# First pass of narrow attention over 64 rows of the array, two heads at a time

## The chip, the cores and the metric

The kernel runs on one core of a Trainium2 chip. The metric is the device time of one execution in microseconds (us). TensorE (PE in the rows, its weight loads PEld) does the matrix products, VectorE (DVE) the reductions, ScalarE (ACT) the exponentials, GpSimd (POOL) small work on SBUF, and SyncE (SP) issues the transfers.

## The reference

Two layers in the macaron form. Each layer has a feed-forward block, an attention block and a feed-forward block. The change touches only the two attentions with 16 heads of 8 dimensions, over 2 sequences of 1024 positions:

```python
scores = einsum('bhqd,bhkd->bhqk', q, k) / sqrt(8)      # first layer, causal
scores = where(causal, scores, -inf)
o = einsum('bhqk,bhkd->bhqd', softmax(scores), v)

att = softmax(einsum('nqd,nkd->nqk', qm, km))           # second layer, not causal
att_out = einsum('nqk,nkd->nqd', att + batch_pos, vm)
```

Everything else (the mixtures of experts, the windowed attention, the norms) is the same before and after.

## The kernel before

A head has only 8 dimensions, so q and k are each cut into three bf16 parts. The products of parts are stacked along the contraction: rows 24i to 24i+23 of `q_slot` hold part i of the queries three times, those of `k_slot` the three parts of the keys, in all 72 rows. Rows 72 to 95 are zero. Rows 96 to 98 hold ones in `k_slot`, and in `q_slot` the negated row maximum in three parts, which a first pass has to find.

Heads are worked on in 8 groups of four. A group has two halves of 512 queries. For a half there are two kinds of work:

- **The first pass.** An item is 128 queries of one head against up to 512 keys: one matmul over 96 rows into one of three banks (`m_bank`, L1463), in the causal stage for the block on the diagonal a second matmul that adds the mask (L1466), then a maximum on DVE (L1529). After the last item of a half DVE negates the maxima (L1538). A "turn" (L1458, a transpose on PE) stands some items later; DVE copies it out (L1525), POOL cuts it into three parts (L1421 to L1427), and three transfers put these into rows 96 to 98 of `q_slot` (L1381).
- **The second pass.** A unit is 128 keys of four heads against up to 512 queries: four scores over 128 rows (L1480), two exponentials on ACT (L1549), in the causal stage a clearing of the diagonal squares on POOL, and four products with the values, each into 32 columns of the array (L1495, fp32, two records each). The first scores of a half wait for the three transfers of its turn.

PE works through a list that is fixed when the program is built. `due(u)` says how many items have been issued before unit u; these are spread among the units. A prologue of items runs before the first unit (49 in the second layer's stage, 62 in the causal one, turns included). An item may be issued when the bank that it wants has been reduced: item m waits for the reductions up to m-3. DVE takes the items in the same order.

SP loads a group's slots with six transfers (`load`), groups 0 to 2 at the start into three slots, later ones when a slot comes free. It also issues `rows` (the three transfers after a turn) and `store` (the result of a half). A transfer that waits holds everything behind it on SP. Group 0 is loaded in the block ahead of the stage, and blocks end with a barrier over all engines.

In the trace the causal stage has the prefix `a1x` (its slots `a1a`), the other `b1x` (`b1a`).

Of the kernel before, what the change touches and what calls it, by code (L numbers as in the profile page):

```python
# [22 lines left out]
NC = 512  # L23
# [1087 lines left out]
class Narrow:  # L1111


    def __init__(self, phase, dram, positions_split):
# [4 lines left out]
        self.k_slot = [phase.sb(f"k_slot{s}", [128, 4, L], BF16) for s in range(3)]  # L1119
        self.v_aug = phase.sb("v_aug", [128, GROUPS, GRANULE_TILES, 128])  # L1120
# [6 lines left out]
        self.slot_loaded = [phase.sem(f"slot_loaded{s}") for s in range(SLOTS)]  # L1127

# [28 lines left out]
    def load(self, sp, group):  # L1157

        n, s = group * 4, group % SLOTS
        for i in range(PARTS):  # L1160
# [6 lines left out]
                         ).then_inc(self.slot_loaded[s], 16)  # L1167

# [113 lines left out]
def narrow_attention(nc, tag, sbuf, dram, narrow, causal):  # L1282
# [16 lines left out]
    for half in range(HALVES):  # L1299
# [5 lines left out]
        for qt in range(4 * qh, 4 * qh + 4):  # L1305
            keys = (qt + 1) * 128 if causal else L
            items += [(half, qt, hh, k0, min(NC, keys - k0)) for k0 in range(0, keys, NC) for hh in (3, 0, 1, 2)]
# [12 lines left out]
    for item in items:  # L1320
        worth.append(worth[-1] + (item[4] + 32 if item[1] is not None else 256))

    def due(u):
# [6 lines left out]
        return max(m for m in range(NI + 1) if worth[m] <= aim)  # L1330

# [10 lines left out]
    for half in range(HALVES):  # L1342
        during = max([u for u in range(NU) if dues[u] <= turn_at[half]], default=-1)
        late = during >= 0 and turn_at[half] - dues[during] >= 2
        cut_after.append(during + 1 if late else during)
    with Phase(nc, tag) as p:
# [3 lines left out]
        q_slot, k_slot, v_aug = narrow.q_slot, narrow.k_slot, narrow.v_aug  # L1350
        probs = [p.sb(f"probs{s}", [128, 4, NC]) for s in range(2)]
# [21 lines left out]
        def _(sp):  # L1373
# [19 lines left out]
            narrow.load(sp, 2)  # L1393
            for half in range(AHEAD):
                rows(half)
            for half in range(HALVES):
# [4 lines left out]
                if half + AHEAD < HALVES:  # L1401
                    rows(half + AHEAD)
                store(half)
# [6 lines left out]
        def _(pool):  # L1410
# [4 lines left out]
            def cut_maxima(half):  # L1415

                into = max_parts[half % 2]
                pool.wait_ge(m_taken, turn_at[half] + 1)
# [26 lines left out]
        def _(pe):  # L1445
            pe.wait_ge(prepared, 2 if causal else 1)

            def first_pass(m):

                half, qt = items[m][0:2]  # L1450
                bank, s = m_bank[m % 3], (half // 2) % SLOTS
                if half % 2 == 0 and m == first_item[half]:
                    pe.wait_ge(slot_loaded[s], 16 * LOADS * (half // 2 // SLOTS + 1))
                if m >= 3:
                    pe.wait_ge(m_taken, m - 2)
                if qt is None:
                    pe.wait_ge(neg_done, half + 1)
                    pe.transpose(bank[0:16, 0:128], neg_max[:, half % 2, :],  # L1458
# [4 lines left out]
                mm = pe.matmul(bank[:, 0:width], q_slot[s][0:MAX_ROW, qt // 4, hh, chunk(qt % 4, 128)],  # L1463
                               k_slot[s][0:MAX_ROW, hh, k0:k0 + width], start=True, stop=not diagonal)
                if diagonal:
                    mm = pe.matmul(bank[:, width - 128:width], ident_bf[:], mask[:, 0, :],  # L1466
# [578 lines left out]
```

## Time and profile before

| | |
|---|---|
| three runs, us | 2774.49, 2777.86 (median), 2784.76 |
| the profiled execution, us | 2785.57, its span 2783.8 |
| mean granted clock of PE | 0.915 of 2.4 GHz |
| causal stage, first and last first-pass matmul | 282.7 and 529.4 |
| second stage, first and last first-pass matmul | 1607.5 and 1971.5 |
| a half in the second stage, as ACT copies results out | 22.9 |
| a group (two halves) in the causal stage | 31.9 |

The two stages take about a quarter of the span. Every term below is read there. The last two lines are distances between starts of the copy of a half's result (L1561).

### The profile page before, as it was taken

To read this page: it belongs to the slowest core of one execution; us is meant where nothing else is said; L and a number is where in the kernel's file an instruction comes from. 1 tells how busy PE (TensorE), PEld (TensorE's weight loads), DVE (VectorE), ACT (ScalarE), POOL (GpSimd) and SP (SyncE) were. 2 spreads that over 40 slices of the span, in tenths; PEclk is the share of its full clock that TensorE was granted. 3 is DMA by queue.
4 is the path that set the end of the run, shared out by engine and by line. 5 is a ranking of instruction groups with operands and counts; after the bars stand their busy time and mean duration, and the time that the engine had idled before them with its cause. 6 is when DMAs were issued, how large, how long until landed. Compare 5 with 4: busy or idle time off the path is not lost. (4 is left out here: it accounts for less than half of the span.)

```text
span 2783.8 us, 38252 instructions
## 1 busy us (share of the span) xinstructions
PE 2443.3 (88%) x11980; PEld 1429.3 (51%) x11980; DVE 2090.0 (75%) x4150; ACT 1427.4 (51%) x3040; POOL 656.4 (24%) x701
## 2 busy tenths in 40 slices
PE   6995899949988999869998589999669899969998
PEld 4773333227756555457775422222136555437776
DVE  3994777538968999279996188888348899639998
ACT  2553356615521777246664136677521477516665
POOL 2334132213317000034443300000005200014443
PEclk8997799969989999879998779999878999969999
DMA  2212111012212000024442611010222000014443
GB/s 65 83 57 75 32 50 47 8 42 104 77 38 50 1 1 1 8 98 156 147 143 58 161 42 33 27 34 9 34 58 46 5 1 1 8 34 145 150 143 120
DMA packets 104848, 166.61 MB, mean 60 GB/s; under 512 B 55170, under 2 KB 77570, under 8 KB 92850
## 3 DMA queue, kind: packets, MB, share of 16 engines
q1 hardware_dynamic: 87812, 162.77, 18.6%
q10 hardware_dynamic: 16896, 2.10, 0.5%
q8 instruction: 73, 1.20, 0.2%
q14 instruction: 67, 0.55, 0.1%
HBM read 145.36 MB, written 12.78 MB: 57 GB/s over the span
## 5 line engine op out<-in xcount | busy, mean ns | idle before, releaser
L1529 DVE TENSOR_REDUCE b1x_maxima<-b1x_m_bank 128x1 f32<-128x512 f32 x512 | 318.9, 682 | 57.5 <-PE b1x_m_bank L1463 56.6
L1549 ACT ACTIVATE b1x_probs<-b1x_e_bank 128x1024 f32<-128x1024 f32 x256 | 248.3, 1021 | 142.0 <-PE b1x_e_bank L1480 141.9
L1529 DVE TENSOR_REDUCE a1x_maxima<-a1x_m_bank 128x1 f32<-128x512 f32 (+3 forms) x384 | 191.3, 548 | 60.3 <-PE a1x_m_bank L1466 31.4
L1549 ACT ACTIVATE a1x_probs<-a1x_e_bank 128x1024 f32<-128x1024 f32 (+1 forms) x192 | 146.1, 813 | 133.4 <-PE a1x_e_bank L1480 133.2
L1463 PE MATMUL b1x_m_bank<-b1a_k_slot,b1a_q_slot 96*128 96x512 bf16 x512 | 186.6, 404 | 11.1 <-DMA b1a_q_slot<-scratch_q_parts 10.8
L1480 PE MATMUL b1x_e_bank<-b1a_q_slot,b1a_k_slot 128*128 128x512 bf16 x512 | 153.6, 383 | 0.9 <-ACT b1x_probs L1549 0.4
L1463 PE MATMUL a1x_m_bank<-a1a_k_slot,a1a_q_slot 96*128 96x512 bf16 (+3 forms) x384 | 121.3, 354 | 21.6 <-POOL a1x_mask L1414 12.8
L1495 PE MATMUL b1x_o_bank<-b1x_probs,b1a_v_aug 128*32 128x512 f32 x1024 | 136.4, 605 | 0.7 <-ACT b1x_probs L1549 0.7
L1463 PEld LDWEIGHTS b1x_m_bank<-b1a_k_slot,b1a_q_slot 96*128 96x128 bf16 x512 | 41.6, 98 | 166.7 <-DVE b1x_maxima L1529 128.8
L632 ACT ACTIVATE g1e_high<-g1e_hidden 128x512 fp32r<-128x512 f32 x128 | 81.0, 633 | 89.9 <-DVE g1e_hidden L665 89.9
L632 ACT ACTIVATE g2e_high<-g2e_hidden 128x512 fp32r<-128x512 f32 x128 | 81.0, 633 | 89.4 <-DVE g2e_hidden L665 89.3
L665 DVE TENSOR_TENSOR g1e_hidden<-g1e_hidden,g1e_share 128x512 f32<-128x512 f32 x128 | 112.9, 882 | 1.2
L665 DVE TENSOR_TENSOR g2e_hidden<-g2e_hidden,g2e_share 128x512 f32<-128x512 f32 x128 | 112.8, 881 | 1.3
L582 PE MATMUL g1e_gate_up<-g_h_high,g1e_w_high 128*128 128x512 f32 x256 | 101.1, 395 | 2.9 <-POOL g1e_w_low L544 2.8
L582 PE MATMUL g2e_gate_up<-g_h_high,g2e_w_high 128*128 128x512 f32 x256 | 101.2, 395 | 2.5 <-POOL g2e_w_low L544 2.5
L582 PE MATMUL g1e_gate_up<-g_h_low,g1e_w_high 128*128 128x512 f32 x256 | 100.5, 392 | 0.0
L582 PE MATMUL g2e_gate_up<-g_h_low,g2e_w_high 128*128 128x512 f32 x256 | 100.3, 392 | 0.0
L582 PE MATMUL g2e_gate_up<-g_h_high,g2e_w_low 128*128 128x512 f32 x256 | 100.2, 391 | 0.0
L582 PE MATMUL g1e_gate_up<-g_h_high,g1e_w_low 128*128 128x512 f32 x256 | 100.1, 391 | 0.0
L1480 PE MATMUL a1x_e_bank<-a1a_q_slot,a1a_k_slot 128*128 128x512 bf16 (+3 forms) x384 | 94.0, 331 | 2.5 <-ACT a1x_probs L1549 1.4
L1463 PEld LDWEIGHTS a1x_m_bank<-a1a_k_slot,a1a_q_slot 96*128 96x128 bf16 x384 | 36.0, 99 | 115.1 <-DVE a1x_maxima L1529 81.2
L224 ACT ACT_TABLE_LOAD x8 | 10.3, 1283 | 165.0 <-PEq L47 165.0
(564 smaller groups left out, 6628.1 us busy)
## 6 DMA issues: line engine op xcount, KB each, us to landing
g1e_share<-scratch_combine SPq DMA_DIRECT2D x32, 1024.0 KB, 4.8
g2e_share<-scratch_combine SPq DMA_DIRECT2D x32, 1024.0 KB, 4.8
f1e_share<-scratch_combine SPq DMA_DIRECT2D x9, 1024.0 KB, 4.8
f2e_share<-scratch_combine SPq DMA_DIRECT2D x9, 1024.0 KB, 4.9
b1e_window<-scratch_bias_table SPq DMA_DIRECT2D x16, 320.0 KB, 4.7
a1a_k_slot<-scratch_k_parts SPq DMA_DIRECT2D x24, 192.0 KB
a1a_q_slot<-scratch_q_parts SPq DMA_DIRECT2D x24, 192.0 KB
b1a_k_slot<-scratch_k_parts SPq DMA_DIRECT2D x24, 192.0 KB
```

Source lines behind the costliest of these rows:

```text
L224: act.activation(dev[:, 0:1], sbuf["mean_w"][:, 0:1], ACT.Sqrt, bias=eps_col[:, 0:1]).then_inc(primed, 1)
L582: mm = pe.matmul(gate_up[j % 2][:, which, :], a[slot][:, at], b[:, chunk(n)], start=(part == 0), stop=(part == 2))
L632: act.activation(high[j % SLOTS][:], hidden[j % SLOTS][:], ACT.Copy).then_inc(high_done, 1)
L665: dve.tensor_tensor(hidden[s][:], hidden[s][:], share[slot][:, chunk(n)], ALU.mult).then_inc(hidden_done, 1)
L1463: mm = pe.matmul(bank[:, 0:width], q_slot[s][0:MAX_ROW, qt // 4, hh, chunk(qt % 4, 128)], k_slot[s][0:MAX_ROW, hh, k0:k0 + width], start=T ...
L1480: mm = pe.matmul(e_bank[pair][:, a, 0:width], k_slot[s][:, hh, chunk(kt, 128)], q_slot[s][:, qh, hh, lo - qh * NC:], start=True, stop=True)
L1495: mm = pe.matmul(o_bank[32 * hh:32 * hh + 32, at:at + width], v_aug[:, half // 2, kt, chunk(hh, 32)], probs[u % 2][:, hh, 0:width], start= ...
L1529: dve.tensor_reduce(maxima[:, k0 // NC, col:col + 1], bank[:, 0:width], AX, ALU.max).then_inc(m_taken, 1)
L1549: act.activation(probs[u % 2][:, 2 * pair:2 * pair + 2, 0:width], e_bank[pair][:, :, 0:width], ACT.Exp, scale=scale).then_inc(exp_done, 1)
```

## The change

The first pass takes only the first 64 rows. Of the nine products of parts it leaves out the last of the keys' parts with the last of the queries' (the maximum is only subtracted, so it need not be exact). The odd heads' first 64 rows are copied by two transfers per group to partitions 64 to 127 of `k_odd` and `q_odd`. An item is now an even and an odd head: two matmuls next to each other in the list, one in the lower 64 rows of the array, one in the upper, into two of the three banks. A pair waits until both its banks have been reduced. In the causal stage the two mask matmuls, still over 128 rows, follow the pair. Within a unit the two pairs of scores now come first, then one pair, the values, and the other pairs of the unit.

```diff
+    def copy_odd(self, sp, group):
+        s = group % SLOTS
+        sp.wait_ge(self.slot_loaded[s], 16 * LOADS * (group // SLOTS + 1))
+        sp.dma_start(self.k_odd[s][64:128, :, :], self.k_slot[s][0:64, 1::2, :]).then_inc(self.odd_loaded[s], 16)
+        sp.dma_start(self.q_odd[s][64:128, ...], self.q_slot[s][0:64, ...][:, 1::2, :]).then_inc(self.odd_loaded[s], 16)
...
-            items += [... for k0 in range(0, keys, NC) for hh in (3, 0, 1, 2)]
+            items += [... for k0 in range(0, keys, NC) for hh in (0, 2)]
-        items.insert(min(last_item[half] + 4, len(items)), (half, None))
+        items.insert(min(last_item[half] + 3, len(items)), (half, None))
...
-        worth.append(worth[-1] + (item[4] + 32 if item[1] is not None else 256))
+        worth.append(worth[-1] + (item[4] + 32 if item[1] is not None else 128))
-        lead = turn_at[AHEAD - 1] + (10 if causal else 14)
+        lead = turn_at[AHEAD - 1] + (5 if causal else 7)
...
             narrow.load(sp, 1)
             narrow.load(sp, 2)
+            narrow.copy_odd(sp, 1)
+            narrow.copy_odd(sp, 2)
...
                 if half + AHEAD < HALVES:
                     rows(half + AHEAD)
+                if SLOTS <= group < GROUPS and half % 2 == 0:
+                    narrow.copy_odd(sp, group)
                 store(half)
...
-                if m >= 3:
-                    pe.wait_ge(m_taken, m - 2)
+                if first_bank[m + 1] > 3:
+                    pe.wait_ge(m_taken, first_bank[m + 1] - 3)
...
-                mm = pe.matmul(bank[:, 0:width], q_slot[s][0:MAX_ROW, ...], k_slot[s][0:MAX_ROW, hh, k0:k0 + width], ...)
+                even = pe.matmul(m_bank[b % 3][:, 0:width], q_slot[s][0:64, ...], k_slot[s][0:64, hh, ...], ...)
+                odd = pe.matmul(m_bank[(b + 1) % 3][:, 0:width], q_odd[s][64:128, ...], k_odd[s][64:128, ...], ...)
                 if diagonal:
-                    mm = pe.matmul(bank[:, width - 128:width], ident_bf[:], mask[:, 0, :], ...)
+                    even = pe.matmul(m_bank[b % 3][:, width - 128:width], ident_bf[:], mask[:, 0, :], ...)
+                    odd = pe.matmul(m_bank[(b + 1) % 3][:, width - 128:width], ident_bf[:], mask[:, 0, :], ...)
...
-                for pair in range(2):
-                    if u + 1 < NU:
+                if u + 1 < NU:
+                    for pair in range(2):
                         scores(u + 1, pair)
-                    if pair < len(share):
-                        first_pass(share[pair])
+                for m in share[:1]:
+                    first_pass(m)
                 values(u)
-                for m in share[2:]:
+                for m in share[1:]:
                     first_pass(m)
...
             narrow.load(sp, 0)
+            narrow.copy_odd(sp, 0)
```

The last two lines stand in both blocks ahead of the stages. Where the second one ends, `bias_out` is stored behind them.

On PE, in the second stage, the list before reads like this from the turn of a half (L1458) on; `m_bank` is the first pass, `e_bank` scores, `o_bank` values. After the last row shown the rows of its unit repeat once, and then come the first scores of the next half:

```order
L1458 MATMUL b1x_m_bank<-ident,b1x_neg_max 16x128
L1480 MATMUL b1x_e_bank<-b1a_q_slot,b1a_k_slot 128x512 x2
L1463 MATMUL b1x_m_bank<-b1a_k_slot,b1a_q_slot 128x512
L1480 MATMUL b1x_e_bank<-b1a_q_slot,b1a_k_slot 128x512 x2
L1463 MATMUL b1x_m_bank<-b1a_k_slot,b1a_q_slot 128x512
L1495 MATMUL b1x_o_bank<-b1x_probs,b1a_v_aug 32x512 x4
L1463 MATMUL b1x_m_bank<-b1a_k_slot,b1a_q_slot 128x512 x2
L1480 MATMUL b1x_e_bank<-b1a_q_slot,b1a_k_slot 128x512 x2
```

After the change it reads like this from the turn (now L1481) on. Behind these rows come one pair, values, one pair, and then the first scores of the next half:

```order
L1481 MATMUL b1x_m_bank<-ident,b1x_neg_max 16x128
L1524 MATMUL b1x_o_bank<-b1x_probs,b1a_v_aug 32x512 x4
L1486 MATMUL b1x_m_bank<-b1a_k_slot,b1a_q_slot 128x512
L1488 MATMUL b1x_m_bank<-b1a_k_odd,b1a_q_odd 128x512
L1509 MATMUL b1x_e_bank<-b1a_q_slot,b1a_k_slot 128x512 x4
```

The turn has moved from behind the values of one unit to ahead of the values of the next one, while the next half's scores have stayed in their unit.

Also on PE, in the second stage, this is the end of a half's last unit after the change, where before three single items stood:

```order
L1524 MATMUL b1x_o_bank<-b1x_probs,b1a_v_aug 32x512 x4
L1486 MATMUL b1x_m_bank<-b1a_k_slot,b1a_q_slot 128x512
L1488 MATMUL b1x_m_bank<-b1a_k_odd,b1a_q_odd 128x512
L1486 MATMUL b1x_m_bank<-b1a_k_slot,b1a_q_slot 128x512
L1488 MATMUL b1x_m_bank<-b1a_k_odd,b1a_q_odd 128x512
L1509 MATMUL b1x_e_bank<-b1a_q_slot,b1a_k_slot 128x512 x4
```

Two pairs stand directly behind each other here. Of the eight units of a half, six have two pairs, the unit of the turn has one and the last unit three.

In the causal stage, on PE, the end of one unit and the scores of the next looked like this before, with the masks (L1466) in between:

```order
L1495 MATMUL a1x_o_bank<-a1x_probs,a1a_v_aug 32x512 x4
L1463 MATMUL a1x_m_bank<-a1a_k_slot,a1a_q_slot 128x512
L1466 MATMUL a1x_m_bank<-a1x_mask,a1x_ident_bf 128x128
L1463 MATMUL a1x_m_bank<-a1a_k_slot,a1a_q_slot 128x512
L1466 MATMUL a1x_m_bank<-a1x_mask,a1x_ident_bf 128x128
L1480 MATMUL a1x_e_bank<-a1a_q_slot,a1a_k_slot 128x256 x2
```

and after the change like this:

```order
L1524 MATMUL a1x_o_bank<-a1x_probs,a1a_v_aug 32x512 x4
L1486 MATMUL a1x_m_bank<-a1a_k_slot,a1a_q_slot 128x512
L1488 MATMUL a1x_m_bank<-a1a_k_odd,a1a_q_odd 128x512
L1492 MATMUL a1x_m_bank<-a1x_mask,a1x_ident_bf 128x128
L1494 MATMUL a1x_m_bank<-a1x_mask,a1x_ident_bf 128x128
L1509 MATMUL a1x_e_bank<-a1a_q_slot,a1a_k_slot 128x256 x4
```

Two products over 96 rows have become two over 64 rows in different halves of the array, and both masks now lie between them and the scores.

## Rows read from the trace of the kernel before

**Rows 1.** The page: busy time, share of the span and instructions of each engine.
```profile
PE 2443.3 (88%) x11980; PEld 1429.3 (51%) x11980; DVE 2090.0 (75%) x4150; ACT 1427.4 (51%) x3040; POOL 656.4 (24%) x701
```

**Rows 2.** Two groups of the causal stage, two halves of the other: busy time by stretch.
```profile
core 0: us, PE busy (x) PEld busy (x) DVE busy (x) ACT busy (x) POOL busy (x), PEclk, DMA share, GB/s
345.80:377.70 31.90, 30.08 (x227) 11.55 (x226) 24.95 (x53) 19.03 (x28) 9.12 (x24) 1.00 0.15 44
...
1661.60:1684.60 23.00, 23.00 (x130) 6.79 (x130) 20.36 (x35) 16.08 (x19) 1.40 (x4) 1.00 0.02 5
```

**Rows 3.** Waits from 1606 to 1976 us: waiter, releaser, total us, times, longest.
```profile
PEld b1x_m_bank L1463 <- DVE b1x_maxima L1529: 128.8, 188, 0.8
DVE b1x_maxima L1529 <- PE b1x_m_bank L1463: 56.6, 91, 18.2
PEld b1x_e_bank L1480 <- DMA b1a_q_slot<-b1x_max_parts: 4.9, 14, 0.4
```

**Rows 4.** Timeline of PE over one unit: start us, us, engine, line, out<-in, count.
```profile
1755.08 0.38 PE L1463 MATMUL b1x_m_bank<-b1a_k_slot,b1a_q_slot 96*128 96x512 bf16 x1
1755.39 1.06 PE L1495 MATMUL b1x_o_bank<-b1x_probs,b1a_v_aug 128*32 128x512 f32 x8
1756.39 0.60 PE L1463 MATMUL b1x_m_bank<-b1a_k_slot,b1a_q_slot 96*128 96x512 bf16 x2
1756.83 0.60 PE L1480 MATMUL b1x_e_bank<-b1a_q_slot,b1a_k_slot 128*128 128x512 bf16 x2
1757.27 0.38 PE L1463 MATMUL b1x_m_bank<-b1a_k_slot,b1a_q_slot 96*128 96x512 bf16 x1
```

**Rows 5.** Timeline of PE in the windowed attention, where 64-row products follow 128-row ones.
```profile
2300.33 0.60 PE L862 MATMUL g2a_scores<-g2a_mask,g2a_ident_bf 128*128 128x512 bf16 x2
2300.86 1.13 PE L867 MATMUL g2a_scores<-g2s_k,g2s_q 64*128 64x256 f32 x8
2301.92 1.08 PE L891 MATMUL g2a_outs<-g2a_probs_T,g2s_v 128*64 128x512 f32 x4
```

**Rows 6.** Timeline of PE and DVE, a first-pass item that DVE had waited for.
```profile
1753.25 0.39 PE L1463 MATMUL b1x_m_bank<-b1a_k_slot,b1a_q_slot 96*128 96x512 bf16 x1
...
1753.67 1.89 DVE L1529 TENSOR_REDUCE b1x_maxima<-b1x_m_bank 128x1 f32<-128x512 f32 x3 [0.41 <-PE b1x_m_bank L1463]
...
1754.42 0.10 PEld L1463 LDWEIGHTS b1x_m_bank<-b1a_k_slot,b1a_q_slot 96*128 96x128 bf16 x1 [0.41 <-DVE b1x_maxima L1529]
```

**Rows 7.** Timeline from a turn to the first scores of the next half.
```profile
1745.02 0.28 PE L1458 MATMUL b1x_m_bank<-ident,b1x_neg_max 128*16 128x128 f32 x1
...
1745.82 0.27 DVE L1525 COPY b1x_rest<-b1x_m_bank 16x128 f32<-16x128 f32 x1
...
1747.36 0.42 POOL L1427 TENSOR_TENSOR b1x_max_parts<-b1x_rest,b1x_max_parts 16x128 bf16<-16x128 f32 x1
...
1747.80 1.83 SPq L1381 DMA_DIRECT2D b1a_q_slot<-b1x_max_parts  x3
...
1750.84 0.11 PEld L1480 LDWEIGHTS b1x_e_bank<-b1a_q_slot,b1a_k_slot 128*128 128x128 bf16 x2 [0.37 <-DMA b1a_q_slot<-b1x_max_parts]
```

**Rows 8.** Weight loads in the second stage's prologue, and the busy time and clock there.
```profile
1610.63 0.10 PEld L1463 LDWEIGHTS b1x_m_bank<-b1a_k_slot,b1a_q_slot 96*128 96x128 bf16 x1 [0.49 <-DVE b1x_maxima L1529]
1611.23 0.10 PEld L1463 LDWEIGHTS b1x_m_bank<-b1a_k_slot,b1a_q_slot 96*128 96x128 bf16 x1 [0.49 <-DVE b1x_maxima L1529]
...
1606.00:1620.00 14.00, 12.53 (x22) 2.26 (x22) 11.91 (x20) 0.00 (x0) 0.00 (x0) 0.50 0.32 98
1620.00:1680.00 60.00, 59.12 (x261) 15.78 (x261) 52.34 (x93) 29.81 (x32) 4.18 (x12) 0.83 0.05 16
```

**Rows 9.** Timeline of the causal prologue: first item, two later ones, first scores.
```profile
282.66 0.29 PE L1463 MATMUL a1x_m_bank<-a1a_k_slot,a1a_q_slot 96*128 96x128 bf16 x1 [12.82 <-POOL a1x_mask L1414]
...
287.77 0.63 PE L1463 MATMUL a1x_m_bank<-a1a_k_slot,a1a_q_slot 96*128 96x512 bf16 x1
...
288.30 0.61 PE L1463 MATMUL a1x_m_bank<-a1a_k_slot,a1a_q_slot 96*128 96x512 bf16 x1
...
310.88 0.26 PEld L1480 LDWEIGHTS a1x_e_bank<-a1a_q_slot,a1a_k_slot 128*128 128x128 bf16 x2 [0.17 <-issue]
```

**Rows 10.** SP's issues at both starts, and the first item of the second stage.
```profile
263.94 0.34 SPq L1161 DMA_DIRECT2D a1a_k_slot<-scratch_k_parts  x1
...
1590.79 0.32 SPq L1161 DMA_DIRECT2D b1a_k_slot<-scratch_k_parts  x1
...
1607.47 6.76 PE L1463 MATMUL b1x_m_bank<-b1a_k_slot,b1a_q_slot 96*128 96x512 bf16 x12 [10.84 <-DMA b1a_q_slot<-scratch_q_parts]
```

More of the change, by code:

```diff
@@ L1119, in __init__ @@
         self.k_slot = [phase.sb(f"k_slot{s}", [128, 4, L], BF16) for s in range(3)]
+        self.q_odd = [phase.sb(f"q_odd{s}", [128, 2, 2, NC], BF16) for s in range(3)]
+        self.k_odd = [phase.sb(f"k_odd{s}", [128, 2, L], BF16) for s in range(3)]
         self.v_aug = phase.sb("v_aug", [128, GROUPS, GRANULE_TILES, 128])
@@ L1127, in __init__ @@
         self.slot_loaded = [phase.sem(f"slot_loaded{s}") for s in range(SLOTS)]
+        self.odd_loaded = [phase.sem(f"odd_loaded{s}") for s in range(SLOTS)]
     def store(self, sp, dst, src, sem):
@@ L1306, in narrow_attention @@
             keys = (qt + 1) * 128 if causal else L
-            items += [(half, qt, hh, k0, min(NC, keys - k0)) for k0 in range(0, keys, NC) for hh in (3, 0, 1, 2)]
+            items += [(half, qt, hh, k0, min(NC, keys - k0)) for k0 in range(0, keys, NC) for hh in (0, 2)]
     last_item = [max(m for m, item in enumerate(items) if item[0] == half) for half in range(HALVES)]
     for half in reversed(range(HALVES)):
-        items.insert(min(last_item[half] + 4, len(items)), (half, None))
+        items.insert(min(last_item[half] + 3, len(items)), (half, None))
     turn_at = [items.index((half, None)) for half in range(HALVES)]
@@ L1330, in due @@
         return max(m for m in range(NI + 1) if worth[m] <= aim)
+    first_bank = [0]
+    for item in items:
+        first_bank.append(first_bank[-1] + (1 if item[1] is None else 2))
     dues = [due(u) for u in range(NU + 1)]
@@ L1343, in narrow_attention @@
         during = max([u for u in range(NU) if dues[u] <= turn_at[half]], default=-1)
-        late = during >= 0 and turn_at[half] - dues[during] >= 2
+        late = during >= 0 and turn_at[half] - dues[during] >= 1
         cut_after.append(during + 1 if late else during)
@@ L1350, in narrow_attention @@
         q_slot, k_slot, v_aug = narrow.q_slot, narrow.k_slot, narrow.v_aug
+        q_odd, k_odd = narrow.q_odd, narrow.k_odd
         probs = [p.sb(f"probs{s}", [128, 4, NC]) for s in range(2)]
@@ L1417, in cut_maxima @@
                 into = max_parts[half % 2]
-                pool.wait_ge(m_taken, turn_at[half] + 1)
+                pool.wait_ge(m_taken, first_bank[turn_at[half] + 1])
                 if half >= 2:
@@ L1462, in first_pass @@
                 diagonal = causal and k0 + width == (qt + 1) * 128
-                mm = pe.matmul(bank[:, 0:width], q_slot[s][0:MAX_ROW, qt // 4, hh, chunk(qt % 4, 128)],
-                               k_slot[s][0:MAX_ROW, hh, k0:k0 + width], start=True, stop=not diagonal)
-                if diagonal:
-                    mm = pe.matmul(bank[:, width - 128:width], ident_bf[:], mask[:, 0, :],
-                                   start=False, stop=True)
-                mm.then_inc(m_done, 1)
+                even = pe.matmul(m_bank[b % 3][:, 0:width], q_slot[s][0:64, qt // 4, hh, chunk(qt % 4, 128)],
+                                 k_slot[s][0:64, hh, k0:k0 + width], start=True, stop=not diagonal)
+                odd = pe.matmul(m_bank[(b + 1) % 3][:, 0:width],
+                                q_odd[s][64:128, qt // 4, hh // 2, chunk(qt % 4, 128)],
+                                k_odd[s][64:128, hh // 2, k0:k0 + width], start=True, stop=not diagonal)
+                if diagonal:
+                    even = pe.matmul(m_bank[b % 3][:, width - 128:width], ident_bf[:], mask[:, 0, :],
+                                     start=False, stop=True)
+                    odd = pe.matmul(m_bank[(b + 1) % 3][:, width - 128:width], ident_bf[:],
+                                    mask[:, 0, :], start=False, stop=True)
+                even.then_inc(m_done, 1)
+                odd.then_inc(m_done, 1)
             def scores(u, pair):
@@ L1790, in _ @@
             narrow.load(sp, 0)
+            narrow.copy_odd(sp, 0)
             sp.wait_ge(out_copied, NT)
```

24 lines of the change are left out of this document (15 added, 9 removed).

## The prediction

> **What bounds the kernel now.** I read the page first. PE is the busiest engine (88%) and DVE the next (75%) [rows 1], but these are averages over stages, so I went to the windows of the two stages that change. In the second stage PE is busy in all of a half's 23.0 us and DVE in 20.4. In the causal stage PE is busy in 30.1 of 31.9 us and DVE in 25.0 [rows 2]. PE's time sets the pace of both. The reader is to see how near DVE is. Its reductions come at a distance of 0.60 us (four reads of rows 8: 1610.63 to 1611.23), so 32 of them need 19.2 us of 22.9. The list of waits says the same: PE's loads waited for DVE 188 times, and DVE for PE 91 times [rows 3]. So PE's time can be taken away only down to some 20 us a half, and only if the two engines hand banks over without loss.
>
> **What the change takes away.** Matmuls of the same kind start 0.216 us apart at 512 columns (0.44 us for two, 1756.39 to 1756.83) [rows 4]. Two 64-row products in different halves of the array do run together: eight of the windowed attention, each as long as a 512-column one, take 1.06 us from the first to what follows (2300.86 to 2301.92) [rows 5], where one after the other they would take 8 x 0.216 = 1.73. Four times 0.216 is 0.86. The other 0.20 is the entry and the exit. So a pair costs 0.216 where its two items cost 0.432. A half has 16 pairs: -3.46 us. A causal group has 24 pairs with 9216 columns in all: at 2.4 columns per ns -3.84 us.
>
> **What it adds on PE.** A change in how the array is divided has a price. From 1755.08 to 1755.39, one product of 96 rows to the first of 32 columns, it takes 0.31 instead of 0.216, so 0.09. Values take 1.00 us from their first to the next first-pass product, of which 0.85 is streaming (four passes over 512 columns) [rows 4]. From 128 to 64 rows, with 128 columns in both, it takes 2300.86 - 2300.33 - 0.43 = 0.10 [rows 5]. The nearest rows for the first weights behind such a switch differ: 0.01 for bf16 (a duration of 0.39 where others show 0.38) [rows 6], about 0.10 for fp32 (the rest of rows 5's 0.20). The pairs are bf16, so I take 0.01 and keep 0.10 as the upper bound. So 0.10 a switch. Before, a unit had two switches, to the values and back. Now it has four: to the pair, to the values, to the second pair, to the scores. The unit of the turn has three. That makes 15 more in a half: +1.5 us. In the causal stage the masks are 128-row products behind the pair, so each such pair between two other kinds adds one more, and two in a row add two. Counted in the program's order, a group goes from 24 to 57 switches: +3.4 us.
>
> The Trainium skill, TensorEngine Tiling (Array Packing), section Theoretical Speedup, promises up to 2x where the contraction has at most 64 rows. By that alone both stages would gain (the sum is in the rival below). The same page, Key Properties, says that a change of mode drains the array; the 0.10 above agrees with that.
>
> **What it adds in waits.** (a) The hand-over. An item that DVE waits for starts on PE at 1753.25 and on DVE at 1753.67, and the load that needed this reduction starts at 1754.42 [rows 6]: 0.42 and 0.75, together 1.17 us. With three banks a pair cannot start before the first reduction of the pair ahead is done, so pairs are at least 1.17 apart. Across values they are 0.23 + 0.09 + 0.88 + 0.10 = 1.30 apart, across scores 0.23 + 0.09 + 0.87 + 0.10 = 1.29, which just fits. Two pairs in a row do not fit: the second waits 1.17 - 0.23 = 0.94, once a half. In front of it nothing can be done by PE, and the next scores, so ACT, wait too. A pair behind the turn needs two reductions: +0.2.
> (b) The turn. From the turn on PE to the next half's first scores pass 5.82 us (1745.02 to 1750.84), and these scores are released by the third of the transfers [rows 7], as in 14 halves [rows 3]. That chain is DVE's copy, POOL's four operations, three issues and the last landing; none of it gets faster. Before, PE's work in between just covered it. Now the turn stands later: behind it come two units of values (1.76), three pairs (0.69), one set of scores (0.87) and the switches (0.7), 4.1 us. DVE is free for the copy some 0.4 sooner. So 5.4 - 4.1 = 1.3 us of wait a half.
> The half comes out at -3.46 + 1.5 + 0.94 + 0.2 + 1.3 = +0.5. Fourteen halves: +7 us.
> (c) The causal loop. Its turns run two halves ahead, so (b) does not arise. (a) does: runs of pairs are more frequent and short ones have small cover. A pair with mask waits longer, for 0.42 is then 0.42 + 0.10 + 0.05. Walking through a group's list with these intervals gives 1.9 us more of waiting than before. -3.84 + 3.4 + 1.9 = +1.4, over some 6.5 groups +9 us.
>
> **The openings.** Nothing covers a pair there. The second stage's prologue ran at a granted clock of 0.50, the lower of the two levels (1.2 GHz), and was bound by DVE at 0.60 an item [rows 8]. At that level 512 columns take 0.43, so 1.17 becomes 1.38 a pair, against 1.20 for two items: 24 pairs, +4.5 us. In the causal prologue (282.7 to 310.9) PE and DVE alternate as the limit; masked items of 512 columns start 0.53 apart (287.77 to 288.30) [rows 9]. A pair with mask needs 0.43 + 0.13 + 0.11 + 0.21 before DVE starts and 0.73 behind that, 1.6 against 1.2; the short ones some 0.9 against 0.45. 22 such pairs at +0.43 and 8 plain ones at +0.18: +10.5. A few units behind the prologues still run at the lower level, where a pair saves 0.43 instead of 0.216: -5 over both.
> The copies add a link to the start. Group 0's load starts at 1590.79, and the first item waited for it until 1607.47 [rows 10], with the bias stores and group 1's load mixed in. SP now waits for it alone, then issues two copies, then the stores, and only then does the block end. I take 13 us for the load, 1.5 for the two issues, 4 for the landing: 1609.5, +2. In the causal stage the start hung on the mask (12.82 us of wait) [rows 9], itself behind a load that began at 263.94; 263.9 + 19 = 283, +1. The bounds of the two copies are 0 (hidden) and 10 us (each as slow as half a load, unhidden).
> Behind both prologues SP copies groups 1 and 2 ahead of `rows`, which waits for group 2's load. That ends later than before by about the copy's time, but PE's prologue is longer too. I count nothing; with no cover it would be up to 5 us a stage.
>
> **The sum.** 7 + 9 + 4.5 + 10.5 - 5 + 3 = +29 us on a profiled time of 2785.6 (span 2783.8 and 1.8 around it), 2814.6. That execution is 7.7 above the median of the three runs, so against the median: 2777.9 + 29 = 2807 us, 1.0% slower. A difference below 0.5% (14 us) could not be told from none.
>
> **The rivals.**
> (F) *Switches between 64 and 128 rows are free* when the columns stay the same. For it speaks only that the 64-row products of rows 5 are fp32 and these are bf16; against it, that the columns there are 128 on both sides and the gap is there all the same. The extra switches are 15 x 14 + 33 x 6.5 = 425, 42 us. Without them 2807 - 42 = 2765, faster. It decides from 0.03 us a switch down, where the sum is nought. If also the waits vanish, DVE's 19.8 us a half is the floor: 14 x 3.1 + 6.5 x 3.8 = 68 gained and the openings' 13 paid, 2723. Chance 0.09. The Trainium skill's "up to 2x", in the section named above, would by itself lead to this end.
> (S) *The waits of (a) and (b) are mostly hidden*, because DVE runs ahead and PE's turn catches an idle DVE. Then 14 x (0.94 + 1.3) = 31 us go: 2776, no change. For it: before, the same chain cost almost nothing (0.4 at most) [rows 3]. Against it: it was covered by 5.8 us of work, and 4.1 are left. Chance 0.18.
> (C) *The clock.* PE does less per us; in the openings it may stay longer at the lower level, or fall to it later. The prologue of rows 8 stayed at 0.50 although PE was busy in 12.5 of 14 us. A half at the lower level costs some 14 us more (17 us of streaming doubled, waits hidden). Two or three of them: +35, 2842. Chance 0.10.
> (W) *Each pair pays the 0.10 of the fp32 rows for its weights.* 14 halves x 14 entries + 6.5 groups x 20 entries = 326, +33 us less what the hand-over hides: 2835. Chance 0.08.
> My own case has the rest, 0.55, with 2792 to 2825 as its range (costs of copies and hand-over at their bounds).
>
> **The numbers.** The range that leaves out no more than 0.2 runs from (S) to between (W) and (C): 2773 to 2840. Slower by over 14 us: my case but its lowest edge, (C) and (W), 0.72. Same: (S) and edges, 0.19. Faster: 0.09.
>
> **What would show it.** The two products of a pair start within 0.02 us of each other. A gap of about 0.1 us stands ahead of each pair and behind it. A half takes 23.4 us, PE shows idle time ahead of the first scores of each half, released by the rows' transfers, of over 1 us, and ahead of the second pair of the last unit of about 0.9, released by DVE. The causal group takes 33.3, its prologue 38 us, the other one 33. The forecast is wrong if no gaps stand at the pairs (F), if the wait for the rows stays below 0.5 (S), or if the clock is below 1.00 inside the loops (C).

## The result and the profile after

The changed kernel takes 2819.89 us (median of 4 runs, 2815.78 to 2826.12), the kernel before beside it 2777.23 (4 runs, 2774.49 to 2784.76): ratio 1.0151, 95% interval 1.0124 to 1.0179: slower, clear of the noise but by less than 2%. The profiled execution took 2819.22 us, its span is 2817.5.

The page has the same row as [rows 1] for after:

```profile
PE 2398.5 (85%) x11980; PEld 1392.6 (49%) x11980; DVE 2103.6 (75%) x4150; ACT 1428.3 (51%) x3040; POOL 657.5 (23%) x701
```

PE is busy 45 us less in a span 34 us longer. Its saved time came back as idle time, and more. The table tells where; each part is read between the starts of the records named (us).

| part | before | after | |
|---|---|---|---|
| causal: block ahead of it, first instruction to first item | 18.7 | 19.5 | +0.8 |
| causal: first item to first scores (prologue) | 28.3 | 38.4 | +10.1 |
| causal: first scores to first result copied | 12.2 | 14.4 | +2.2 |
| causal: first to last result (group: 31.88, 33.14) | 236.4 | 244.5 | +8.1 |
| second: block ahead of it to first item | 51.6 | 53.9 | +2.3 |
| second: prologue | 28.7 | 33.3 | +4.6 |
| second: first scores to first result | 25.5 | 25.9 | +0.4 |
| second: first to last result (half: 22.92, 23.31) | 336.6 | 340.9 | +4.3 |
| both stages | 738.0 | 770.8 | +32.8 |

The span grew by 33.7, so 0.9 is left for all blocks that the change doesn't touch.

The windows that answer to [rows 2], a causal group and a half:

```profile
365.00:398.20 33.20, 29.01 (x227) 9.55 (x227) 25.29 (x53) 18.97 (x27) 9.17 (x24) 1.00 0.22 58
1733.60:1756.90 23.30, 21.17 (x131) 5.35 (x129) 20.82 (x36) 15.98 (x19) 1.39 (x4) 1.00 0.04 7
```

PE (third number) used to fill a half and now leaves 2.1 us of it empty. In the group the empty part goes from 1.8 to 4.2 us. DVE's busy time is what it was. The end of a half's last unit, with two pairs in a row, and the unit behind it, on PE (start, us, operation):

```profile
1756.63 0.39 PE L1486 MATMUL b1x_m_bank<-b1a_k_slot,b1a_q_slot 64*128 64x512 bf16 x1
1756.63 0.39 PE L1488 MATMUL b1x_m_bank<-b1a_k_odd,b1a_q_odd 64*128 64x512 bf16 x1
1757.80 0.39 PE L1486 MATMUL b1x_m_bank<-b1a_k_slot,b1a_q_slot 64*128 64x512 bf16 x1 [0.78 <-DVE b1x_maxima L1560]
1757.80 0.39 PE L1488 MATMUL b1x_m_bank<-b1a_k_odd,b1a_q_odd 64*128 64x512 bf16 x1
1758.12 1.04 PE L1509 MATMUL b1x_e_bank<-b1a_q_slot,b1a_k_slot 128*128 128x512 bf16 x4
1759.09 0.39 PE L1486 MATMUL b1x_m_bank<-b1a_k_slot,b1a_q_slot 64*128 64x512 bf16 x1
...
1759.41 1.07 PE L1524 MATMUL b1x_o_bank<-b1x_probs,b1a_v_aug 128*32 128x512 f32 x8
1760.41 0.39 PE L1486 MATMUL b1x_m_bank<-b1a_k_slot,b1a_q_slot 64*128 64x512 bf16 x1
...
1762.02 1.07 PE L1524 MATMUL b1x_o_bank<-b1x_probs,b1a_v_aug 128*32 128x512 f32 x8
```

The two products of a pair start in the same 0.01 us and end together. What follows them starts 0.32 later, 0.216 of streaming and 0.10 for the switch. From values to values a unit takes 2.61 us (1759.41 to 1762.02); before it took 2.84 (1755.39 [rows 4] to the next values at 1758.23). So units do gain, 0.23 us each. Two pairs in a row stand 1.17 apart (1756.63 to 1757.80), the second with an idle PE ahead of it. The other loss stands at the first scores of each half:

```profile
1776.03 0.39 PE L1486 MATMUL b1x_m_bank<-b1a_k_slot,b1a_q_slot 64*128 64x512 bf16 x1
...
1777.66 1.04 PE L1509 MATMUL b1x_e_bank<-b1a_q_slot,b1a_k_slot 128*128 128x512 bf16 x4 [1.24 <-DMA b1a_q_slot<-b1x_max_parts]
```

The list of waits of the second stage (1600 to 2030 us) has both in sum, beside [rows 3]:

```profile
PEld b1x_m_bank L1486 <- DVE b1x_maxima L1560: 167.2, 219, 1.5
DVE b1x_maxima L1560 <- PE b1x_m_bank L1488: 54.3, 33, 19.2
PE b1x_m_bank L1486 <- DVE b1x_maxima L1560: 29.4, 37, 1.0
PEld b1x_e_bank L1509 <- DMA b1a_q_slot<-b1x_max_parts: 22.0, 15, 1.5
PE b1x_e_bank L1509 <- DMA b1a_q_slot<-b1x_max_parts: 17.0, 14, 1.2
```

17.0 us in 14 halves is 1.2 us of idle PE each. The load of weights waited for the same rows 0.4 us at most before.

The second stage's prologue, where nothing covers a pair, first on PE and then as a window, whose third number from the end is the granted clock:

```profile
1656.37 0.61 PE L1486 MATMUL b1x_m_bank<-b1a_k_slot,b1a_q_slot 64*128 64x512 bf16 x1 [0.79 <-DVE b1x_maxima L1560]
...
1657.76 0.60 PE L1486 MATMUL b1x_m_bank<-b1a_k_slot,b1a_q_slot 64*128 64x512 bf16 x1 [0.78 <-DVE b1x_maxima L1560]
```

```profile
1618.90:1666.70 47.80, 20.27 (x67) 3.60 (x67) 32.29 (x53) 5.16 (x5) 1.69 (x5) 0.50 0.43 110
```

Pairs are 1.39 us apart. SP's queue at that stage's start, and the first item:

```profile
1612.13 0.73 SPq L1167 DMA_DIRECT2D b1a_q_slot<-scratch_q_parts  x1
1622.48 0.69 SPq L1176 DMA_DIRECT2D b1a_k_odd<-b1a_k_slot  x1
1623.22 0.66 SPq L1177 DMA_DIRECT2D b1a_q_odd<-b1a_q_slot  x1
...
1627.77 0.61 PE L1486 MATMUL b1x_m_bank<-b1a_k_slot,b1a_q_slot 64*128 64x512 bf16 x1 [11.76 <-POOL b1x_ident_bf L1433]
```

SP stood 9.6 us behind its last load until this had landed, and the copies follow. The releaser named for the first item is a copy on POOL at the start of the block (it ended at 1627.71), because the block itself begins late.

### The profile page after: what moved, and what is told of

It reads as the page before. It is cut to its first block and busy times, and to the rows that moved or that the text cites. A ratio compares the mean times of both kernels' runs of the same rounds, so it can differ in the third digit from the quotient of the medians.

```text
span 2817.5 us, 38290 instructions
## 1 busy us (share of the span) xinstructions
PE 2398.5 (85%) x11980; PEld 1392.6 (49%) x11980; DVE 2103.6 (75%) x4150; ACT 1428.3 (51%) x3040; POOL 657.5 (23%) x701
## 5 line engine op out<-in xcount | busy, mean ns | idle before, releaser
L1560 DVE TENSOR_REDUCE b1x_maxima<-b1x_m_bank 128x1 f32<-128x512 f32 x512 | 326.8, 685 | 59.2 <-PE b1x_m_bank L1488 54.3
L1509 PE MATMUL b1x_e_bank<-b1a_q_slot,b1a_k_slot 128*128 128x512 bf16 x512 | 135.6, 386 | 17.9 <-DMA b1a_q_slot<-b1x_max_parts 17.0
L1486 PE MATMUL b1x_m_bank<-b1a_k_slot,b1a_q_slot 64*128 64x512 bf16 x256 | 104.4, 408 | 42.6 <-DVE b1x_maxima L1560 29.4
L1486 PEld LDWEIGHTS b1x_m_bank<-b1a_k_slot,b1a_q_slot 64*128 64x128 bf16 x256 | 23.9, 93 | 200.7 <-DVE b1x_maxima L1560 167.2
L1486 PE MATMUL a1x_m_bank<-a1a_k_slot,a1a_q_slot 64*128 64x512 bf16 (+2 forms) x192 | 68.9, 359 | 52.6 <-DVE a1x_maxima L1560 38.3
L1488 PE MATMUL b1x_m_bank<-b1a_k_odd,b1a_q_odd 64*128 64x512 bf16 x256 | 104.4, 408 | 0.0
L658 DVE TENSOR_TENSOR g1e_hidden<-g1e_gate_up,g1e_gated 128x512 f32<-128x512 f32 x128 | 87.1, 680 | 6.8 <-ACT g1e_gated L614 6.8
```

The lines of the kernel that those rows point to most:

```text
L658: dve.tensor_tensor(hidden[s][:], gate_up[j % 2][:, 1, :], gated[s][:], ALU.mult).then_inc(product_done, 1)
L1486: even = pe.matmul(m_bank[b % 3][:, 0:width], q_slot[s][0:64, qt // 4, hh, chunk(qt % 4, 128)], k_slot[s][0:64, hh, k0:k0 + width], start= ...
L1488: odd = pe.matmul(m_bank[(b + 1) % 3][:, 0:width], q_odd[s][64:128, qt // 4, hh // 2, chunk(qt % 4, 128)], k_odd[s][64:128, hh // 2, k0:k0 ...
L1509: mm = pe.matmul(e_bank[pair][:, a, 0:width], k_slot[s][:, hh, chunk(kt, 128)], q_slot[s][:, qh, hh, lo - qh * NC:], start=True, stop=True)
L1560: dve.tensor_reduce(maxima[:, k0 // NC, col:col + 1], m_bank[(b + odd) % 3][:, 0:width], AX, ALU.max).then_inc(m_taken, 1)
```

## The experiments

The medians of the kernel before, run beside them, were 2780.16 (13 runs, for 1 to 4), 2783.88 (23, for 5 to 8) and 2777.75 (17, for 9 to 11). Where only one time is given, the kernel ran once, and its parts are read from that execution's profile. A half and a group are given as in the table above.

**1. The price of a switch.** The kernel before, single items, 64 rows instead of 96.

```diff
-    pe.matmul(bank[:, 0:width], q_slot[s][0:MAX_ROW, ...], k_slot[s][0:MAX_ROW, hh, k0:k0 + width], ...)
+    pe.matmul(bank[:, 0:width], q_slot[s][0:64, ...], k_slot[s][0:64, hh, k0:k0 + width], ...)
```

> The kernel before, whose first pass reads 64 rows instead of 96 and nothing else: same order, same columns, one head at a time (the last part of the keys times the last of the queries is left out of the maximum, as in the change). Theory (a switch between 128 and 64 rows costs PE 0.10 us): a unit of the second stage goes from two switches to six, 8 x 4 x 0.10 = +3.3 us a half, 26.2 instead of 22.9; the causal group gains about 80 switches, 40 instead of 31.9; the whole kernel is 90 to 110 us slower than before. Rival (the switch is free, the change loses only by its order and its waits): a half stays at 22.9, the group at 31.9, the time within 3 us of before.

Measured: 2878.69 us, span 2876.9; half 26.05, group 36.44. On PE, in one unit:

```profile
1821.04 0.60 PE L1463 MATMUL b1x_m_bank<-b1a_k_slot,b1a_q_slot 64*128 64x512 bf16 x2
1821.58 0.60 PE L1480 MATMUL b1x_e_bank<-b1a_q_slot,b1a_k_slot 128*128 128x512 bf16 x2
1822.12 0.39 PE L1463 MATMUL b1x_m_bank<-b1a_k_slot,b1a_q_slot 64*128 64x512 bf16 x1
```

Two products and what follows them are 0.54 apart, where [rows 4] have 0.44. A half has 48 switches instead of 16 and takes 3.13 us longer: 0.098 each. Rival (F) is out. The group came out 3.6 under what I had expected: its 72 added switches cost 4.56 us, 0.063 each. That some stand where PE waited for DVE anyway is my reading; no run shows it.

**2. Pairs without the array's halves.** The changed kernel's order, copies and waits, but each pair as two products over 96 rows from the slots.

```diff
-    even = pe.matmul(m_bank[b % 3][:, 0:width], q_slot[s][0:64, ..., hh, ...], ...)
+    even = pe.matmul(m_bank[b % 3][:, 0:width], q_slot[s][0:MAX_ROW, ..., hh, ...], ...)
-    odd = pe.matmul(..., q_odd[s][64:128, ..., hh // 2, ...], k_odd[s][64:128, ...], ...)
+    odd = pe.matmul(..., q_slot[s][0:MAX_ROW, ..., hh + 1, ...], k_slot[s][0:MAX_ROW, hh + 1, ...], ...)
```

> The changed kernel with both products of a pair over 96 rows of the slots, one behind the other: the order, the pairs, the banks and the copies stay, the division of the array goes. Theory: a half gets back 3.46 us of streaming and loses 1.5 of switches, and the waits for the turn (1.3) and the third pair (0.9) shrink by a quarter: about 24.8 against 23.3, so 96 rows in this order are slower than 64. The prologues stay long (33 us and at least 38), since it is the hand-over of two banks out of three that sets them. Rival (it is the division of the array that loses, the order costs nothing): a half goes back to 22.9, the prologues to 28.7 and 28.3.

Measured: 2833.46 us; half 24.35, group 34.04, prologues 33.7 and 41.4. The prologues stay long although no product is in the array's upper half: it is the taking of two banks at a time that makes them long. The half's 24.35 against 22.92 is the price of order and waits (1.4 us), and the two rows of products side by side give back 1.0 of it, with the price of their own switches (1.5 us) already in. I had expected 24.8, so the order costs 0.45 less than I thought.

**3. The turn one place earlier**, in the second stage alone.

```diff
-        items.insert(min(last_item[half] + 3, len(items)), (half, None))
+        items.insert(min(last_item[half] + (3 if causal else 2), len(items)), (half, None))
-        lead = turn_at[AHEAD - 1] + (5 if causal else 7)
+        lead = turn_at[AHEAD - 1] + (5 if causal else 8)
```

> The changed kernel with the turn of the second stage one pair earlier, so that it stands behind the values of a half's fifth unit; the causal stage as it is, the prologue has 25 items as before. Theory (the chain from the turn is 1.2 to 1.3 us longer than what covers it): a half takes 22.0 to 22.2 instead of 23.3, PE's wait for the rows' transfers falls from 17.0 us in 14 times to under 3, the kernel gets 15 to 18 us faster than the changed one. Rival (the wait only moves, to DVE or to the third pair): a half stays at 23.0 or more.

Measured: 2796.58 us; half 22.12, that is 1.19 less than the changed kernel's. The wait is gone where it was:

```profile
PE b1x_e_bank L1509 <- DMA b1a_q_slot<-b1x_max_parts: 2.9, 14, 0.2
```

**4. Even units too**: the turn counts for nothing when items are spread over units, so no unit gets a third pair.

```diff
-        worth.append(worth[-1] + (item[4] + 32 if item[1] is not None else 128))
+        worth.append(worth[-1] + (item[4] + 32 if item[1] is not None else (128 if causal else 0)))
```

> The same as the one with the early turn, and a turn now counts nothing when items are spread, so that every unit of the second stage has two pairs and none three. Theory: the 0.94 us ahead of the third pair and the 0.2 behind the turn go, 0.4 comes back where a pair follows a turn: a half takes 21.2 to 21.5. With the causal stage unchanged (21 us slower than before) the whole comes to about 4 us above before or within 5 of it. Rival (DVE is the limit by now): a half does not get below 22.

Measured: 2794.33 us (10 runs, 2784.58 to 2802.74), ratio to before 1.0048 (1.0024 to 1.0072). The half is 21.65, 0.47 less than in run 3, and not the 21.2 to 21.5 that I had expected. The 0.78 us of idle time ahead of the third pair and the 0.22 ahead of the next half's scores are gone, but the pair behind the turn, which needs two reductions, now finds PE idle for 0.49 us (at 1778.48, released by DVE). DVE is busy in 21.06 of the 21.65 us by then and PE in 21.16, so neither has much left to give. In the second stage pairs now gain 1.27 us a half. The causal stage (314.5 us, 18.8 more than before) takes it all back.

**5. Pairs in the second stage alone.** The causal stage as before, with single items and no copies; the second stage as in 4.

```diff
+    paired = lambda item: item[1] is not None and not causal and item[0] >= SINGLES    # SINGLES = 0
+            heads = (3, 0, 1, 2) if causal or half < SINGLES else (0, 2)
...
+                if not paired(items[m]):
+                    mm = pe.matmul(m_bank[b % 3][:, 0:width], q_slot[s][0:MAX_ROW, ...], k_slot[s][0:MAX_ROW, ...], ...)
```

> The causal stage goes back to single heads over 96 rows with no copies of odd heads; the second stage keeps pairs over 64 rows, with the even units and the early turn of the run before. Theory (in the causal stage nothing of the change pays, neither in its loop, where the hand-over of banks and the switches around masks eat the streams saved, nor in its prologue): the causal stage falls back to 295.6 us with a group of 31.9, the second stage stays at 431 to 433 with a half of 21.6 to 21.7, and the span is 10 to 12 us below that of the kernel before, a ratio of 0.995 to 0.998 in the medians. Rival (what the changed kernel lost in the causal stage comes from something both stages share, such as the clock that falls and comes back later in the prologue): the second stage gets worse by some 5 us when the causal stage is as before, or the causal stage stays over 300 us.

Measured: 2771.06 us (12 runs), ratio 0.9962 (0.9941 to 0.9984). The causal stage took 295.8 (group 31.89), the second 431.5 (half 21.65): 10.7 less than before over both. The profiled span is 18.6 less; the other 8 lie in blocks that are the same in both kernels, so the 10.7 is what the change can be credited with.

**6. Single items in the second stage's prologue.** As 5 with `SINGLES = 1`: the first half's 32 items are single, and the 8 pairs of the next half that end the prologue stay pairs. Group 0's copy is issued behind the loads of group 1 within the stage:

```diff
+            narrow.load(sp, 1)
+            narrow.copy_odd(sp, 0)
+            narrow.load(sp, 2)
```

> As the run with pairs in the second stage alone, and there too the first half's items (the prologue and the first items of the loop) are single heads over 96 rows, with the copy of the first group's odd heads issued behind the next loads. Theory (the prologue is paced by the hand-over of bank pairs at the low clock, 1.39 us for a pair against 1.05 to 1.1 for two single items, and the copy delays the first item by the time of its two issues and landing): the second stage's prologue falls from 33.3 to 28.7 to 29.5, its opening from 54 to 51.6, the stage from 431.5 to 424 to 426, and the span is 16 to 19 below that of the kernel before, a ratio of 0.993 to 0.995. Rival (the prologue is long because of the low clock alone, or the copy costs nothing): the prologue stays over 31, or the opening stays at 54, and the ratio is that of the run before.

Measured: 2768.52 us (12 runs), ratio 0.9952 (0.9927 to 0.9978). The start came down to 50.6, but the prologue went up to 35.0, where I had expected 28.7 to 29.5. SP and PE show why:

```profile
1641.82 0.59 SPq L1180 DMA_DIRECT2D b1a_k_odd<-b1a_k_slot  x1
...
1643.10 2.68 SPq L1407 DMA_DIRECT2D b1a_q_slot<-b1x_max_parts  x3
...
1647.35 1.49 PE L1527 MATMUL b1x_e_bank<-b1a_q_slot,b1a_k_slot 128*128 128x512 bf16 x3 [4.60 <-DMA b1a_q_slot<-b1x_max_parts]
```

The turn stood at 1632.7, and POOL had its parts ready at 1635.6. Its rows were issued at 1643.1, behind the copy of group 2, which waited for that group's loads. PE had finished all its items at 1642.8, 30.5 us behind the first, and waited 4.6 us. That is the cover I had named in the prediction ("with no cover it would be up to 5 us a stage"). Two things took it away: the items ended 3.2 us sooner than the prologue of run 5 (33.7), and the rows were issued 30.8 us behind the first item instead of 28.0, because group 0's copy now stood among the loads.

**7 and 8. No masks in the first pass**, in the changed kernel and in the kernel before: the maximum is then taken over the whole of a diagonal block. Both have the one line

```diff
-                diagonal = causal and k0 + width == (qt + 1) * 128
+                diagonal = False
```

> The changed kernel without the causal masks in the first pass: the maximum is taken over the whole of a diagonal block (the second pass keeps its masks), so that no product over 128 rows stands between the pairs. Theory (in the causal loop the masks and the switches around them are what makes a group 1.3 us longer than before): a group falls from 33.14 to 29.5 to 30.2, the causal loop from 244.5 to some 220 to 225. Set beside the kernel before without the same masks, the pairs then gain or stand level: a group of at most 0.2 over its. Rival (the group is set by the hand-over of bank pairs, or by VectorE, whatever stands on TensorE): the group falls by under 1.5 us, and stays over 1 us longer than that of the kernel before without masks.

> The kernel before without the causal masks in the first pass (the maximum over the whole diagonal block), to set beside the changed kernel without them. Both theories: 16 masks over 128 columns fall away for each group, about 0.9 us of streams and as much of loads at most that aren't hidden, so the group falls from 31.88 to 30.0 to 30.8 and the causal loop from 236.4 to some 224 to 229. The theory of the switches around masks then wants the changed kernel's group within 0.2 of this one; the theory of the hand-over wants it over 1 us longer.

Two groups (7) and two groups (8) from window to window; PE's busy time is the third number:

```profile
391.96:453.57 61.61, 52.21 (x382) 15.54 (x388) 49.80 (x106) 37.82 (x53) 18.42 (x48) 1.00 0.24 63
```

```profile
377.30:439.48 62.18, 56.88 (x384) 18.79 (x388) 49.68 (x106) 38.04 (x54) 18.28 (x48) 1.00 0.15 45
```

A group takes 30.81 with pairs (7) and 31.09 without them (8). So masks cost the pairs 2.33 us a group and the single items 0.79; the difference of 1.54 is more than the 1.26 that the changed kernel loses. But pairs only draw level: they save 3.84 of streaming and keep 0.28 of it. PE idles 4.7 us of a group there, 2.7 in the other kernel. The expected upper edges were too low by 0.6 for 7 and by 0.3 for 8. The prologue without masks takes 34.1 against 28.1.

**9. The rows ahead of the copy.** As 6, with SP's order changed:

```diff
+            rows(0)
             narrow.copy_odd(sp, 2)
```

> As the run whose second stage begins with single items, but SyncE sends the first half's rows of maxima before it copies the third group's odd heads (there the rows stood behind that copy, which waited for the third group's loads until 1641.8 us, and the first scores waited 4.6 us for the rows). Theory (single items do make the prologue shorter, and the queue took it back): the first pass ahead of the scores ends 30.5 us after it began, so the prologue falls from 35.0 to 30.5 to 31, the stage from 429.8 to 425 to 427, and the ratio to the kernel before is 0.993 to 0.996. Rival (the rows are late by the transfers themselves, which run beside the second and third groups' loads): the prologue stays over 33.5.

Measured: 2761.46 us (12 runs, 2750.39 to 2775.83), ratio 0.9937 (0.9913 to 0.9961), the fastest kernel with pairs. The prologue takes 30.8. The intervals of 5, 6 and 9 overlap; over both stages their profiles have 727.3, 724.4 and 723.3 us (738.0 before).

```profile
1617.00 2.01 SPq L1407 DMA_DIRECT2D b1a_q_slot<-b1x_max_parts  x3
...
1621.89 0.66 SPq L1180 DMA_DIRECT2D b1a_k_odd<-b1a_k_slot  x1
...
1624.05 0.13 PEld L1528 LDWEIGHTS b1x_e_bank<-b1a_q_slot,b1a_k_slot 128*128 128x128 bf16 x2 [0.44 <-DMA b1a_q_slot<-b1x_max_parts]
```

**10 and 11. Shorter reductions**, over half the columns of a bank (the maximum leaves out the other half), in the changed kernel and in the kernel before. A reduction of 128x256 takes 0.42 us, one of 128x512 0.68.

```diff
-  dve.tensor_reduce(maxima[...], m_bank[(b + odd) % 3][:, 0:width], AX, ALU.max)
+  dve.tensor_reduce(maxima[...], m_bank[(b + odd) % 3][:, 0:width // 2], AX, ALU.max)
```

> The changed kernel with a reduction over half the columns of each bank (the maximum leaves out the other half), so that a bank comes back some 0.25 us earlier, with the same products and the same order on TensorE. Theory (the pairs pay with waits for the hand-over of banks, TensorE's 3.3 us of a causal group and all of the prologues' 1.39 us for a pair, and the rest with switches): the prologues fall to 26 to 30 in the second stage and 32 to 35 in the causal one, a group falls by 1.5 to 2.5 to 30.6 to 31.6, and a half, where only the third pair of some units and the turn wait for VectorE, by 0.3 to 1.0 to 22.3 to 23.0. Rival (switches and the order on TensorE set the loops alone): group and half fall by under 0.4.

> The kernel before with the same shorter reduction, to set beside the changed kernel with it. Theory (single items, with three banks for them, wait little for VectorE in the loops: 1.2 us of a group): a group falls by 0.3 to 1.0 and a half by under 0.5; the prologue of the second stage, where a reduction starts each 0.595 us, falls from 28.7 to 26 to 28, by what TensorE at its low clock allows. The rival (VectorE is the bound of both kernels alike) has group and half fall by as much as in the changed kernel.

Measured: 2782.92 and 2751.83 us. The half is 22.74 (10) and 22.80 (11), the group 31.09 and 30.11. In the second stage this is as the theory has it: the changed kernel's half falls by 0.57, the other's by 0.12, and then they are level. In the causal stage the changed kernel's group falls by 2.05, as expected, but the other's by 1.77, not by at most 1.0: DVE holds back both loops there. Most of that didn't show as idle time of PE, which waited for DVE only 0.75 us a group (the list is in the next section): with the same products PE's busy time in a group fell from 30.08 to 28.94. In run 10 the items of the second stage's prologue took 26.8 us, and then PE waited 5.7 for the rows, which I had not foreseen. In run 11 it was 17.4 and 7.4, together 24.8 where I had expected 26 to 28.

## Why the prediction was right

The forecast was 2807 us, 29 more than before, with 2792 to 2825 as the range of its own case; 2820 came, 43 more than the median beside it. By its own steps:

- **Pairs run side by side, a switch costs 0.10.** Both products start together, and run 1 measured 0.098 a switch. The Trainium skill, TensorEngine Tiling (Array Packing), Theoretical Speedup, gives up to 2x; the two products have it, a unit of the loop 2.84 / 2.61 = 1.09. Rivals (F) and (W) fall: a unit by the terms of the sum has two pairs, scores, values and four switches, 2.56 us, and takes 2.61, so weights cost at most 0.03 a pair, not 0.10.
- **(a) The hand-over.** 1.17 between pairs, as said, and 0.78 of idle time at the third, where I had 0.94. It is now also shown as a cause, by runs 2, 4 and 10.
- **(b) The turn.** 1.3 was expected, PE idles 1.2, and run 3, which only moves the turn, gave back 1.19. Rival (S) falls.
- **The half** came out at +0.39 (forecast +0.5), all halves at +4.3 (+7). **The group** at +1.26 (+1.4), the causal loop at +8.1 (+9). Its terms hold roughly one by one. The lists of waits from 330 to 530 us, of the kernel before and of the changed one, have

```profile
PE a1x_m_bank L1463 <- DVE a1x_maxima L1529: 4.7, 18, 0.4
```

```profile
PE a1x_m_bank L1486 <- DVE a1x_maxima L1560: 19.9, 42, 0.8
```

That is 0.75 and 3.3 us a group, +2.55 where I had 1.9. With -3.84 of streams and a total of +1.26 it leaves 2.55 for the 33 added switches, 0.08 each.
- **The prologues**: +4.6 (+4.5) and +10.1 (+10.5; its own parts, 22 at 0.43 and 8 at 0.18, make 10.9). **The starts**: +2.3 (+2) and +0.8 (+1).
- **The step that failed** is "A few units behind the prologues still run at the lower level, where a pair saves 0.43 instead of 0.216: -5 over both." How many units these are was taken from no row. First scores to first result took 2.6 us more over both stages, not 5 less. In the kernel before, the clock rose 1.7 us behind the first scores of the causal stage and 4.2 behind those of the second, and in that time PE had no first-pass product in the one and a single one in the other: there was next to nothing to save. In the changed kernel it rose 8.1 and 5.8 us behind them, and three pairs stood there in all, worth 1.3 us at 0.43 each. Causal stage, before and after, with the granted clock as the third number from the end:

```profile
311.00:312.70 1.70, 1.70 (x6) 0.44 (x4) 0.90 (x2) 0.62 (x1) 0.00 (x0) 0.51 0.04 7
```

```profile
317.40:324.90 7.50, 7.14 (x28) 1.59 (x26) 2.41 (x5) 3.56 (x4) 1.63 (x4) 0.50 0.00 0
...
325.50:330.00 4.50, 3.84 (x35) 1.34 (x33) 4.02 (x9) 1.73 (x5) 2.30 (x7) 1.00 0.01 2
```

How late the clock rises differs from execution to execution. In runs 3 and 4, whose causal stage is the changed kernel's, it rose 4.2 and 4.3 us behind the first scores, and the first result came after 12.9 us instead of 14.4 (before: 12.2). In run 7, with the same second stage, it rose after 3.3, and the result came after 24.5 instead of 25.9 (before: 25.5). So the 5 is not there in any of them, and the 2.6 is in good part that of the one profiled execution. This is rival (C) in small: only in the openings, 7.6 us off (2.6 and 5), and in the loops the clock stayed at 1.00, but for 3.4 us near the end of the causal stage (from 550.8), which the kernel before has too (from 534.5).
- **The rest**. The stages give +32.8 in place of +29: the opening's 7.6 too little was in part offset by the loops, which came 3.6 under their 16. That two errors of opposite sign met is luck. The medians differ by 42.7 and the profiled times by 33.7, because the profiled execution of before was some 8 us above its median and that of after was not. I carried the 29 over to the median unchanged. Blocks that the change doesn't touch spread by more than that: they took 2029.8 us (run 9) to 2056.7 (run 6) in the profiled executions. So some 10 of the 42.7 us are in no part that was read here.

Open is how the causal loop's time divides. With short reductions the changed kernel's group is still 0.98 longer, without masks 0.28 shorter; so masks with their switches weigh more than the hand-over, but the two overlap, and no run takes both away. Nor was a fourth first-pass bank tried.

## What to carry to other kernels

Two products in two halves of the array's rows take two banks at once, so with three banks the pairs of an unbroken row are apart by product plus reduction (1.17 us here), whatever PE saves. Count the switches in the order the program really has, at 0.10 us each, and look where the products are already spaced by work of the other kind: there pairs pay (half 22.92 to 21.65), in an uncovered prologue or between masks they don't. A shorter piece of work on the busiest engine moves what was timed by it: turn and rows had to move too, and SP's order after them. Run 11 says that the reductions themselves were the larger prize: 0.26 us off each is worth some 26 us to the kernel before (one execution, 25.6 of it in the two stages), though no way to get the full maximum in that time was tried.

## What the runs showed of the hardware

**With shorter reductions the granted clock of the prologue rose.** In the kernel before the second stage's prologue ran at 0.50 throughout [rows 8]. It did so too in runs 1 and 8, which have the same order there. With the shorter reduction (run 11) and nothing else changed, it rose within the prologue:

```profile
1578.90:1590.00 11.10, 11.03 (x32) 3.02 (x32) 10.43 (x30) 0.00 (x0) 0.00 (x0) 0.84 0.39 108
1590.00:1596.00 6.00, 5.59 (x19) 1.65 (x18) 5.93 (x20) 0.00 (x0) 1.40 (x4) 1.00 0.20 78
1596.00:1603.70 7.70, 0.33 (x1) 0.16 (x3) 0.88 (x3) 0.00 (x0) 0.00 (x0) 0.73 0.14 53
```

PE did the 49 products of the prologue in 17.4 us, busy in 11.03 of the first 11.10, where the kernel before needed 28.9 for them. When it then stood idle for 7.4 us (third row, waiting for the rows of the turn), the clock fell again. From the first causal item to the last rise the same edit left 9.9 us at the lower level instead of 26.6, and that prologue took 21.9 us instead of 28.3. With pairs the shorter reduction did not do it: in run 10, where PE was busy in 14.89 of 27.00 us, the second stage's prologue stayed at 0.50. Each of these is one execution.

**A copy from SBUF to SBUF waits longest for its source.** SP's wait for the loads ahead of the two copies took 9.6 us and the two issues 1.4. From issue to landing the second stage's `k_odd` copies took 3.2 us (median; 3.1 to 4.4) and its `q_odd` copies 3.7 (3.7 to 10.8). The first item came 4.6 us behind the start of the second issue.
